# Cross-attention with two softmaxes: probabilities divided by their sums before or after the value products

## What is computed

```python
q = rms_norm(linear(x, q_w, q_b), norm_q_w)
k, v = rms_norm(linear(ctx_txt, k_w, k_b), norm_k_w), linear(ctx_txt, v_w, v_b)
k_img, v_img = rms_norm(linear(ctx_img, k_img_w, k_img_b), norm_k_img_w), linear(ctx_img, v_img_w, v_img_b)
img_x = attention(q, k_img, v_img)        # softmax over 257 keys
txt_x = attention(q, k, v)                # softmax over 118 keys
out = linear(txt_x + img_x, o_w, o_b)
# x = x + out; then a layer norm, a gate over 8 experts (top 2), three-layer experts, and a second residual
```

## Time and profile before

| | us |
|---|---|
| median of 3 runs (lowest to highest) | 901.93 (901.48 to 904.78) |
| the profiled execution, its own time | 902.71 |
| its span, first to last instruction | 900.9 |
| TensorE busy in the span | 766.8 (85%) |
| VectorE busy | 569.9 (63%) |
| ScalarE busy | 451.1 (50%) |
| GpSimd busy | 156.6 (17%) |

### The profile page before, as it was taken

One profiled execution on the slowest core, in us unless ns is written; L12 is line 12 of the kernel. 1 busy time (PEld: TensorE's weight loads), 2 busy tenths in 40 slices (PEclk: granted clock), 3 DMA queues, 4 the chain that ended last, 5 costly groups with the idle time before them and its releaser, 6 DMA issues.

```text
span 900.9 us, 17483 instructions
## 1 busy us (share of the span) xinstructions
PE 766.8 (85%) x6238; PEld 679.6 (75%) x6238; DVE 569.9 (63%) x1033; ACT 451.1 (50%) x1020; POOL 156.6 (17%) x228
## 2 busy tenths in 40 slices
PE   2989999999999997640499999999999999999920
PEld 2767777777777775430499999999999999999920
DVE  4767686767676755462166767675767676767625
ACT  3455656566566665530155545454546454545410
POOL 2423333334343322116100000000000000000024
PEclk9999999999999997655599999999999999999965
DMA  6770202111010003057345656465656575646578
GB/s 226 279 287 1 67 11 66 36 42 56 22 56 22 11 23 152 31 178 258 100 142 209 222 187 235 171 235 179 238 186 244 186 243 177 230 177 236 183 249 251
DMA packets 33982, 137.53 MB, mean 153 GB/s; under 512 B 3712, under 2 KB 3728, under 8 KB 22928
## 3 DMA queue, kind: packets, MB, share of 16 engines
q1 hardware_dynamic: 31200, 129.23, 41.3%
q0 software_dynamic: 2736, 7.69, 3.1%
HBM read 115.36 MB, written 21.54 MB: 152 GB/s over the span
## 4 chain that ended last, share of the span: by engine, by line
PE 72%; DVE 14%; issue 5%; DMA 3%; ACT 3%; POOL 1%; SPq 1%; ACTq 0%; DVEq 0%; POOLq 0%
PE tiles L982 7%; PE tiles L983 7%; PE tiles L984 7%; PE scores L1239 4%; PE scores L1241 4%; PE scores L1240 4%; PE ptb L1092 4%; PE pvb L1116 3%; PE ptb L982 3%; PE ptb L984 3%; PE ptb L983 3%; PE pvb L984 3%; PE pvb L983 3%; PE pvb L982 3%; PE scores L1083 2%
## 5 line engine op out<-in xcount | busy, mean ns | idle before, releaser
L798 DVE TENSOR_TENSOR w<-scr,w 128x2048 fp32r<-128x2048 f32 x76 | 174.6, 2297 | 83.5 <-ACT w L593 83.5
L593 ACT ACTIVATE w<-scr 128x2048 fp32r<-128x2048 f32 x76 | 144.9, 1909 | 63.8 <-PE scores L1241 59.3
L582 ACT ACTIVATE scr<-ptb 128x336 f32<-128x336 f32 x128 | 59.8, 467 | 96.6 <-PE ptb L1092 95.7
L518 POOL DMA_INDIRECT scr<-slots_d,slotu x16 | 15.2, 952 | 444.5 <-SPq L393 440.0
L982 PE MATMUL tiles<-c,w 128*128 128x256 f32 (+1 forms) x272 | 81.8, 301 | 3.9 <-DVE c L940 2.6
L982 PE MATMUL tiles<-w 128*128 128x256 f32 x288 | 81.5, 283 | 0.0
L983 PE MATMUL tiles<-w 128*128 128x256 f32 x288 | 81.5, 283 | 0.0
L984 PE MATMUL tiles<-w 128*128 128x256 f32 x288 | 81.5, 283 | 0.0
L983 PE MATMUL tiles<-c,w 128*128 128x256 f32 (+1 forms) x272 | 79.1, 291 | 0.0
L984 PE MATMUL tiles<-c,w 128*128 128x256 f32 (+1 forms) x272 | 79.0, 291 | 0.0
L1092 PE MATMUL ptb<-ident,scr 112*128 112x112 f32 x384 | 63.3, 276 | 9.4 <-ACT scr L582 9.4
(11 more groups left out here) (215 smaller groups left out, 2173.3 us busy)
## 6 DMA issues: line engine op xcount, KB each, us to landing
scr<-in_dram SPq DMA_DIRECT2D x86, 1024.0 KB, 4.8
slots_d<-xr SPq DMA_DIRECT2D x3, 2048.0 KB, 17.4
scr<-in_dram SPq DMA_DIRECT2D x8, 750.0 KB, 4.7
scr<-slots_d SPq DMA_DIRECT2D x10, 512.0 KB, 4.6
slots_d<-scr SPq DMA_DIRECT2D x9, 512.0 KB, 3.8
xn<-in_dram SPq DMA_DIRECT2D x10, 256.0 KB, 4.7
xb<-in_dram SPq DMA_DIRECT2D x8, 224.0 KB, 2.7
xr<-in_dram SPq DMA_DIRECT2D x8, 224.0 KB, 2.5
```

The source lines that it names most:

```text
L582: act.activation(probT[:, h % 8, :, :], ptb[:, 0:KT * L].rearrange("p (t q) -> p t q", t=KT), ACT.Copy).then_inc(S["pt_done"], 1)
L593: act.activation(EH[slot], raw[slot], ACT.Copy).then_inc(S["eh_done"], 1)
L798: dve.tensor_tensor(EL[slot], raw[slot], EH[slot].bitcast(F32), ALU.subtract).then_inc(S["el_done"], 1)
```

## The change

Each head's probabilities are divided by their sums before they are transposed. `invert_sums` runs for each head in step h + 1 on VectorE: two reciprocals, then the text part (118 columns) is multiplied in place. ScalarE multiplies the image part (257 columns) in place with the image's reciprocal (`normalise`), also in step h + 1. `transpose` waits for both. `attend` then makes one accumulation over the three key tiles with 12 matmuls; the transposes of the reciprocals, `take_sums`, `rx`, `rbc`, `pvn` and `vx` are gone, and `attended` is one addition of the bias. The projected value of the last image row is written by the DMA into row 0 of `vn` tile 2 itself, after that tile's evacuation.

Several things change their places with it. The transposes of x move from step 0 to step 5, between two quarters of "o" and behind the text keys. The third key chunk "k3" is evacuated at the start of step 10 on ScalarE. `add_squares` is cut in two: two sums ahead of `attended` in step 10, the last one behind it. The low halves of the keys are made ahead of `attended`. The gate's product goes ahead of the projection work of step 15 on TensorE, and the gate logits ahead of `ln_apply` and `split_ctx_low` on VectorE. The value products no longer wait for "ms" and the like by `pv_read` but by `a_done`.

```diff
--- before.py
+++ after.py
@@ -44,12 +44,12 @@
 BIG = ("k0", "k1", "kt", "o", "qt", "k2", "k3", "v0", "v1", "v2")
-FILL = {0: [("xT", 0, 1), ("k0", 0, 4)], 1: [("k1", 0, 4)], 2: [("kt", 0, 2)], 3: [("kt", 2, 4)], 4: [("o", 0, 2), ("kx", 0, 1)],
-        5: [("o", 2, 4)], 6: [("qt", 0, 2)], 7: [("qt", 2, 4)], 8: [("k2", 0, 4), ("q", 0, 1)], 9: [("k3", 0, 4)],
+FILL = {0: [("k0", 0, 4)], 1: [("k1", 0, 4)], 2: [("kt", 0, 2)], 3: [("kt", 2, 4)], 4: [("o", 0, 2), ("kx", 0, 1)],
+        5: [("o", 2, 3), ("xT", 0, 1), ("o", 3, 4)], 6: [("qt", 0, 2)], 7: [("qt", 2, 4)], 8: [("k2", 0, 4), ("q", 0, 1)], 9: [("k3", 0, 4)],
         10: [("v0", 0, 2)], 11: [("v0", 2, 4), ("ms", 0, 1)], 12: [("v1", 0, 2)], 13: [("rb", 0, 1), ("v1", 2, 4)],
...
-EVACUATE_AT = {1: ["k0", "xT"], 2: ["k1"], 4: ["kt"], 8: ["qt"], 9: ["k2"], 10: ["k3"], 12: ["v0"], 13: ["rb"], 14: ["v1"]}
+EVACUATE_AT = {1: ["k0"], 2: ["k1"], 4: ["kt"], 5: ["xT"], 8: ["qt"], 9: ["k2"], 12: ["v0"], 13: ["rb"], 14: ["v1"]}
 CHUNKS = [range(0, 4), range(4, 8)] + [range(8 + 2 * i, 10 + 2 * i) for i in range(4)]
...
@@ -292,9 +290,8 @@
-                    if b > 1:
-                        sp.wait_ge(S["pv_ready"], NC * (b - 1))
-                    sp.dma_start(vx[0:1, p, :], vlast_d[b:b + 1, :]).then_inc(vrow_in[p], 16)
+                    taken(sp, "v2", b - 1)
+                    sp.dma_start(vn[p][0:1, 2, :], vlast_d[b:b + 1, :]).then_inc(vrow_in[p], 16)
                 if has_prep(b):
...
@@ -567,12 +563,16 @@
                     act.wait_ge(S["t_ready"], NH * b + h - 3)
-                if not (fixed(b, 0) and h < 8):
-                    act.wait_ge(S["rsum_done"], NC * b + h // 4 - 1)
                 act.activation(probs[0:L, s, 0:IMG], scores[0:L, s, 0:IMG], ACT.Exp,
-                               bias=nmax[0:L, g, s, 0:1], accum_out=sums[0:L, g, 0, s:s + 1])
+                               bias=nmax[0:L, g, s, 0:1], accum_out=sums[0:L, g, s, 0:1])
                 act.activation(probs[0:L, s, IMG:KEYS], scores[0:L, s, IMG:KEYS], ACT.Exp,
-                               bias=nmax[0:L, g, s, 1:2], accum_out=sums[0:L, g, 1, s:s + 1]).then_inc(S["exp_done"], 1)
+                               bias=nmax[0:L, g, s, 1:2], accum_out=sums[0:L, g, s, 1:2]).then_inc(S["exp_done"], 1)
+            def normalise(b, h):
+                s, g = h % 4, (h // 4) % 2
+                act.wait_ge(S["inverted"], NH * b + h + 1)
+                act.activation(probs[0:L, s, 0:IMG], probs[0:L, s, 0:IMG], ACT.Copy,
+                               scale=rsum[0:L, g, s, 0:1]).then_inc(S["normal_img"], 1)
...
@@ -596,17 +591,19 @@
                         split_weights(WEIGHTS_AT[h])
+                    if h == 10 and has_prep(b):
+                        evacuate("k3", b, p)
                     if h % 4 and has_heads(b):
                         weigh(b, p, h)
+                    if h == 0 and has_tail(b):
+                        normalise(b - 1, NH - 1)
+                    if h and has_heads(b):
+                        normalise(b, h - 1)
                     if h < LAG:
...
                         take_transposed(b, h - LAG)
-                    if h == 2 and has_tail(b):
-                        take_sums(b - 1, 3)
-                    if h in (6, 10, 14) and has_heads(b):
-                        take_sums(b, (h - 6) // 4)
                     if h == 0 and has_heads(b):
...
@@ -749,12 +745,12 @@
-            def add_squares(b):
-                dve.wait_ge(S["squares"], (NC + 2) * (b + 2) - 1)
-                dve.tensor_tensor(sq[:, 0, :], sq[:, 0, :], sq[:, 2, :], ALU.add).then_inc(S["sum_a"], 1)
-                dve.wait_ge(S["squares"], (NC + 2) * (b + 2))
-                dve.tensor_tensor(sq[:, 1, :], sq[:, 1, :], sq[:, 3, :], ALU.add).then_inc(S["sum_a"], 1)
+            def add_squares(b, i):
+                dve.wait_ge(S["squares"], (NC + 2) * (b + 2) - 1 + i)
+                dve.tensor_tensor(sq[:, i, :], sq[:, i, :], sq[:, i + 2, :], ALU.add).then_inc(S["sum_a"], 1)
+            def add_sums(b):
                 dve.wait_ge(S["sum_a"], 2 * (b + 2))
@@ -773,21 +769,19 @@
-            def invert_sums(b, g):
-                dve.wait_ge(S["exp_done"], NH * b + 4 * g + 4)
-                if not (fixed(b, 0) and g < 1):
-                    dve.wait_ge(S["pv_ready"], NC * b + g)
-                dve.reciprocal(rsum[0:L], sums[0:L, g % 2, :, :]).then_inc(S["inverted"], 1)
-                dve.wait_ge(S["inverted"], NC * b + g + 1)
-                dve.tensor_copy(rx[0:L], rsum[0:L].unsqueeze(3).to_broadcast([L, 2, 4, HD])).then_inc(S["rsum_done"], 1)
+            def invert_sums(b, h):
+                dve.wait_ge(S["exp_done"], NH * b + h + 1)
+                s, g = h % 4, (h // 4) % 2
+                dve.reciprocal(rsum[0:L, g, s, :], sums[0:L, g, s, :]).then_inc(S["inverted"], 1)
+                dve.wait_ge(S["inverted"], NH * b + h + 1)
+                dve.tensor_scalar(probs[0:L, s, IMG:KEYS], probs[0:L, s, IMG:KEYS], rsum[0:L, g, s, 1:2], None,
+                                  ALU.mult).then_inc(S["normal_txt"], 1)
...
-                dve.wait_ge(S["rb_done"], NC * b + g + 1)
-                dve.tensor_tensor(pvn[:, :], pvb[:, 0:2 * L], rbc[:, :], ALU.mult).then_inc(S["pv_read"], 1)
-                dve.wait_ge(S["pv_read"], NC * b + g + 1)
-                dve.scalar_tensor_tensor(af[:, :], pvn[:, 0:L], vbias[:, g:g + 1], pvn[:, L:2 * L], ALU.add, ALU.add).then_inc(S["a_done"], 1)
+                dve.wait_ge(S["pv_ready"], NC * b + g + 1)
+                dve.tensor_scalar(af[:, :], pvb[:, 0:L], vbias[:, g:g + 1], None, ALU.add).then_inc(S["a_done"], 1)
@@ -805,35 +799,39 @@
                         dve.memset(probs[:, :, KEYS:KT * P], 0.0)
+                    if h == 0 and has_tail(b):
+                        invert_sums(b - 1, NH - 1)
+                    if h and has_heads(b):
+                        invert_sums(b, h - 1)
                     if h % 4 == 0 and has_heads(b):
...
                         maxima(b, h // 4, 1)
-                    if h == 1 and has_tail(b):
-                        invert_sums(b - 1, 3)
-                    if h in (5, 9, 13) and has_heads(b):
-                        invert_sums(b, (h - 5) // 4)
                     if h == 14 and has_prep(b):
...
                         split_keys_low(b + 1, 1 - p, 0)
+                    if h in KEYS_LOW_AT and has_heads(b):
+                        split_keys_low(b, p, KEYS_LOW_AT[h])
+                    if h == 10 and has_prep(b):
+                        add_squares(b, 0)
+                        add_squares(b, 1)
                     if h in (6, 10, 14) and has_heads(b):
                         attended(b, (h - 6) // 4)
+                    if h == 10 and has_prep(b):
+                        add_sums(b)
                     if h in (7, 11, 15) and has_heads(b):
...
                         normalise_keys(p if step else 1 - p, c)
-                    if h in KEYS_LOW_AT and has_heads(b):
-                        split_keys_low(b, p, KEYS_LOW_AT[h])
                     if h == 2 and has_tail(b):
...
                         split_ctx_low(b + 2, 1)
-                    if h == 1 and has_prep(b):
-                        take_x(b)
                     if h == 5 and has_prep(b):
                         take_kx(b, p)
+                        take_x(b)
                     if h == 6 and has_tail(b):
@@ -844,8 +842,6 @@
                         ln_apply(b, x1[0:L, :], x1, mv2, rs2, "ln2", "xg_done")
-                    if h == 10 and has_prep(b):
-                        add_squares(b)
                     if h == 11 and has_prep(b):
@@ -854,12 +850,12 @@
                         normalise_keys(1 - p, 0)
+                    if h == 15 and has_tail(b):
+                        dve.wait_ge(S["gate_ready"], b)
+                        dve.tensor_tensor(lg[0:L, b - 1:b, :], pvb[0:L, 0:E].unsqueeze(1), bgr[0:L, :].unsqueeze(1), ALU.add).then_inc(S["lg_done"], 1)
                     if h == 15 and has_prep(b + 1):
...
                         split_ctx_low(b + 3, 0)
-                    if h == 15 and has_tail(b):
-                        dve.wait_ge(S["gate_ready"], b)
-                        dve.tensor_tensor(lg[0:L, b - 1:b, :], pvb[0:L, 0:E].unsqueeze(1), bgr[0:L, :].unsqueeze(1), ALU.add).then_inc(S["lg_done"], 1)
                     if h == 15 and has_tail(b) and not fixed(b, DONE):
@@ -990,16 +986,13 @@
                         pe.wait_ge(S["xn_done"], n + 1)
-                        if b > 1:
-                            pe.wait_ge(S["lg_done"], b - 1)
-                        if b > 0:
-                            pe.wait_ge(S["pv_read"], NC * b - 1)
+                        pe.wait_ge(S["kx_read"], b + 2)
                     else:
...
                         if has_heads(b):
-                            pe.wait_ge(S["pv_read"], NC * b + (name == "q"))
-                    if name != "xT":
```

(43 more changed lines are left out.)

17 lines of the change are left out of this document (5 added, 12 removed).

## The result

The changed kernel takes 897.87 us as a median of 9 runs (894.30 to 898.74), the kernel before 904.38 beside it (901.48 to 906.10, 9 runs). The ratio is 0.993, 95% interval 0.9915 to 0.9945: 6.5 us less, where 24 were forecast. The profiled execution took 894.30 us, span 892.5, the lowest of the nine; it is 8.4 shorter in span than the one before.

A forecast was written before the change was run, and what follows sets the result against it. TensorE was taken as nearly the bound in repeating batches, the chain between engines in the last. Gains of 11.2 + 2.1 + 1.5 + 8.0 + 1.3 = 24.1 us gave 878 us against the median, range 865 to 895.

The forecast's parts named there:

- The value products: On TensorE, one pass, two transposes and most of a handover go: 0.4 us a group, 11.2 us for 28 groups.
- The prices of the new operations: ScalarE's multiplication taken at 0.36 us; VectorE's reciprocal and multiplication together at 0.45 a head.
- No wait is left before the squares: In repeating batches, TensorE's wait of 0.93 us a batch before the sums of squares goes.
- The expert loop: Half of the run, not touched by the change; forecast to be as long as before.
- gaps given back, 1.6 a batch: New TensorE waits around the batch boundary: 11.2 us in seven batches, against 13.3 removed, net 2.1 gained.
- my sum: The forecast's added-up gains: products 11.2, gaps 2.1, clock 1.5, last batch 8.0, start 1.3, together 24.1 us.
- rival 1: VectorE's boundary between batches becomes the bound: 3.2 us a batch given back, no clock gain, 890 us; chance 0.22.
- the last batch, 8.0: Last batch: shorter cycles of 7.3 us save 5.8, an earlier and shorter end 2.2; bounds 4 and 10.
- the start, 1.3: At the start, key projections go ahead of x's transposes on TensorE: 1.3 us gained, bounds 0 and 2.5.
- Clock, 1.5: TensorE's granted clock should fall less often in repeating batches, where three falls are shown: 1.5 us gained.

The follow-up runs named there:

- the three early steps: Changed kernel with VectorE's inversions for heads 13 and 15 and the third group's attended part moved ahead; batches 41.2 us, median 4 us better by the ratios.
- the products alone with attended early: Changed kernel without multiplications and reciprocals, third group's attended part ahead of the low halves; batch 39.29 us, only the attention stretch is read.
- moving its head: On top of the three early steps, ScalarE evacuates the spread norms earlier in step 13; batches 40.5 us, 0.8 gained.
- unloading it: ScalarE instead of GpSimd makes the high half of the context's image columns; batches gained 0.3 on the changed kernel alone, 0.4 on top of other changes.
- the swap on ScalarE: On the fastest kernel so far, ScalarE evacuates ahead of multiplying in steps 1 and 13, VectorE scales x behind head 0's inversion; batches 39.3 us, 0.3 gained.
- taking x out of it: x transposed in step 3, ahead of the text keys: 0.7 a batch and 6.7 us on the changed kernel alone, 0.7 and 10.5 on top of others.

## Why the prediction was wrong

**Right.** The value products: 0.38 a group. The prices of the new operations: ScalarE's multiplication has its successor 0.40 us later (0.36 taken), VectorE's pair takes 0.39 from start to start where nothing is beside it (0.45 taken). No wait is left before the squares. The expert loop is as it was.

**Wrong: gaps given back, 1.6 a batch.** Between two undisturbed batches, 1.5 of products, 0.94 before the sums, 0.69 at the split of x and 0.2 before x's transposes are removed, 3.35 together (my sum has 3.5); the batch is 0.16 shorter. So 3.2 were given back, the very number of rival 1. 1.95 of it stands in five waits: head 13 (0.53) and the gate product (0.44), which the sum had at nothing; the value products for x (0.39) and x for the text keys (0.20), together 0.59 for my 0.25; head 0 (0.39, of my 0.7). The rest is in gaps too short for the list, like 0.24 before the first key projection (of my 0.35), and some 1.0 of it has no name. Cut at the first scores, the first key projection and the product that spreads the norms, the undisturbed batch from 257.6 us was 1.52 + 32.44 + 7.55 and is 1.22 + 31.44 + 8.69. Given back are 0.25, 1.4 and 1.5: the last piece, which runs beside VectorE's chain, has grown by 1.1 though 0.38 of products was taken out of it. With head 0, which is in the middle piece, 2.2 of the 3.2 are at VectorE's boundary, as rival 1 had it; the other 1.0 is in the middle, most of it with x. VectorE's own part is as long as before, 7.4 us from the scaling of the queries to the split's end (0.2 more was forecast). What the step missed is that it begins later against TensorE, since ScalarE evacuates the norms behind one multiplication more (1.66 us behind the product in place of 1.27). That a chain of the same length also turns into waits because TensorE has less work beside it is argued from this and fits the longer last piece; no run shows it by itself. I had asked what is added to the chain, and not what was hiding it. And I priced each wait for itself, where the experiments showed a ring: removed waits of 1.36 us a batch gave 0.1, and only moving its head (0.8), unloading it (0.3 to 0.4), the swap on ScalarE (0.3) or taking x out of it (0.7) gave anything. The price of all divisions in this ring is the difference of the three early steps and the products alone with attended early: 41.24 and 39.29, 1.95 us a batch, though no engine is busy all of that time.

**Wrong: the last batch, 8.0.** It gave 4.6: 4.3 in the cycles, where 5.8 were forecast, and 0.3 behind them in place of 2.2. The cycles are 7.41, 7.73 and 8.50, and I had 7.3: multiplications there wait for VectorE's reciprocals up to 1.2 us, once because the gate logits stand ahead of them. The granted clock over the last batch is 0.63, and was 0.71, which the sum left out. The last group takes 1.5 longer from its scores to its value products (12.7 and 11.2). From there to the low half of the attended part it is 1.8 shorter, near the forecast's 2.2, although GpSimd's conversion meets VectorE's for 2.1 us.

**Wrong: the start, 1.3.** It costs 1.8 in the profiled run, and 3 more where the clock stays low (52 in place of 49 in kernels that start alike). I counted when TensorE could begin and not what it would then stand for, nor that the clock could fall behind that.

**Clock, 1.5.** Right in kind, and most of what the batches gained. Two batches of the kernel before and two of the changed one, first a repeating batch with a lower clock and then the first batch:

```profile
129.00:172.52 43.52, 41.17 (x390) 33.41 (x390) 30.97 (x74) 26.32 (x96) 15.02 (x23) 0.96 0.13 40
47.25:85.83 38.58, 34.58 (x325) 27.42 (x326) 25.14 (x58) 24.24 (x92) 13.21 (x18) 1.00 0.38 144
```

```profile
132.58:174.46 41.88, 39.83 (x349) 30.71 (x348) 33.28 (x91) 31.17 (x108) 14.56 (x23) 0.99 0.14 45
49.01:89.83 40.82, 35.20 (x295) 27.25 (x295) 28.70 (x80) 28.87 (x102) 13.01 (x19) 0.96 0.35 129
```

Before, three repeating batches had 0.96 and took 43.2 to 43.6 us; now two have 0.99 and 0.97 and take 41.9. That is 4.7 us gained beyond the 0.16 a batch. But the first batch lost 2.2, with its clock at 0.96 in place of 1.00, which no part of the sum had. The second batch is long at a clock of 1.00 in both kernels (43.17 and 42.75). So 2.5 of the 3.7 us come from these two, and the rest is little more than the 0.16 a batch. In the kernel before, two of the three falls came behind the 0.9 us wait before the sums, within 2 us, as the prediction reads them; the third, at 301 us, came at the end of a wait of 0.79 before the transposes of x. The same 0.9 us wait ended at 117, 202 and 287 us without a fall, and no run here tells why.

## What to carry to other kernels

When work is added to engines that form a ring, ask first when the ring's slowest stretch begins, that is what now stands in each queue ahead of its first step, and only then what is inside it. A list of waits is a list of places where slack ends, not of prices: take one away in a trial and see whether the same time comes back under another name before counting it. An engine that is sent ahead of its inputs gains less than it starts sooner: here TensorE began 4.8 us sooner, stood 4.3 us for what it needed next and then ran some microseconds at half its clock.

## What the runs showed of the hardware

Unexpected was that less work can be slower: a wait of 1.8 us on TensorE was followed by a granted clock of 0.54 over the next 4 us, and taking the wait away made a batch 3 us shorter. Such a fall doesn't follow each wait of about 1 us, as the kernel before shows. And VectorE's two-input conversion in SBUF (2.3 us) held up GpSimd for its whole length, not only a conversion there (0.28 us took 2.40) but the issue of an indirect DMA too (0.95 became 2.38 beside one of them, 6.79 beside three).
